# A post-norm attention and feed-forward layer on one Trainium2 core: turning tiles in quadrants of 32 on VectorE in place of TensorE transposes

## The reference

```python
local  = softmax(mask(q k^T / 4)) v                       # window of 128, per head
pooled = x.reshape(B, 64, 8, D).mean(axis=2)              # chunk means
lat    = softmax(mask(rq rk^T / 4)) rv                    # 64 latents, 4 heads
remote = lat @ rout_w + rout_b
gate   = sigmoid(local @ gl_w + remote_h @ gr_w)          # one value per token and head
mixed  = gate * local + (1 - gate) * remote_h
x1 = layernorm(x + mixed @ out_w + out_b)
h  = gelu(ternary_linear(x1, w_up))                       # rms norm, ternary weights
y  = layernorm(x1 + ternary_linear(h, w_down))
```

## Time and profile before

| | us |
|---|---|
| median of 3 runs | 1155.28 |
| lowest, highest | 1149.62, 1156.93 |
| the profiled execution: its own time | 1154.15 |
| the profiled execution: its span | 1152.4 |

### The profile page before, as it was taken

One profiled execution on the slowest core, in us unless ns is written; L12 is line 12 of the kernel. 1 busy time (PEld: TensorE's weight loads), 2 busy tenths in 40 slices (PEclk: granted clock), 3 DMA queues, 4 the chain that ended last, 5 costly groups with the idle time before them and its releaser, 6 DMA issues.

```text
span 1152.4 us, 37627 instructions
## 1 busy us (share of the span) xinstructions
PE 1019.2 (88%) x15616; PEld 642.4 (56%) x15616; DVE 902.5 (78%) x2119; ACT 682.4 (59%) x1076; POOL 698.0 (61%) x874
## 2 busy tenths in 40 slices
PE   5878999999999999999999999999999999986855
PEld 2445565655556565655656565565656555564533
DVE  6688888887887988787888888788788878875445
ACT  2425666656666665666666565666666566664523
POOL 7216675656667576566757565566756565673744
PEclk9889999999999999999999999999999999996877
DMA  7740604325060423416061331616042250600000
GB/s 219 204 125 14 193 21 120 87 77 148 32 193 23 145 61 104 121 42 182 24 167 56 113 94 59 166 33 187 28 131 77 85 139 33 174 23 20 2 19 18
DMA packets 46662, 108.18 MB, mean 94 GB/s; under 512 B 7542, under 2 KB 26486, under 8 KB 43382
## 3 DMA queue, kind: packets, MB, share of 16 engines
q1 hardware_dynamic: 46348, 105.78, 31.9%
q10 hardware_dynamic: 144, 0.00, 0.0%
HBM read 71.58 MB, written 34.08 MB: 92 GB/s over the span
## 4 chain that ended last, share of the span: by engine, by line
PE 44%; DVE 28%; ACT 16%; issue 5%; POOL 3%; DMA 2%; SPq 1%; DVEq 0%; POOLq 0%; ACTq 0%
PE oacc L1459 8%; PE work L1537 7%; PE oacc L1480 6%; PE work L1398 5%; PE scores L1439 4%; ACT Pt L792 4%; PE work L1469 3%; DVE Pt L974 3%; DVE nmax L1048 3%; DVE x L1111 2%; DVE rem L1115 2%; PE scores L1377 2%; ACT hbuf L828 2%; PE work L1403 2%; DVE oT L1176 2%
## 5 line engine op out<-in xcount | busy, mean ns | idle before, releaser
L792 ACT ACTIVATE Pt<-scores 128x1024 f32<-128x1024 f32 (+1 forms) x256 | 228.6, 915 | 104.5 <-PE oacc L1459 63.8
L1048 DVE TENSOR_REDUCE nmax<-work 128x3 f32<-128x480 f32 x352 | 218.1, 637 | 25.2 <-PE work L1403 20.0
L656 POOL TENSOR_TENSOR h_lo<-hbuf,h_hi 128x512 f16<-128x512 f32 x128 | 148.2, 1158 | 130.7 <-DVE h_hi L1170 130.7
L628 POOL TENSOR_SCALAR_AFFINE_SELECT Pt<-Pt 128x512 f32<-128x512 f32 x256 | 166.8, 652 | 91.2 <-ACT Pt L792 90.0
L615 POOL TENSOR_TENSOR parts<-Pt,parts 128x512 bf16<-128x512 f32 x64 | 72.9, 1157 | 138.2 <-ACT parts L728 138.2
L1459 PE MATMUL oacc<-Pt,Vp 128*32 128x256 f32 (+1 forms) x2048 | 150.2, 360 | 5.8 <-DVE ytok L1192 2.7
L1398 PE MATMUL work<-Ks,Qs 98*32 98x160 bf16 x4096 | 139.8, 235 | 11.4 <-DVE nmax L1048 7.4
L1439 PE MATMUL scores<-Qs,Ks 100*32 100x160 bf16 (+4 forms) x4096 | 114.8, 230 | 23.5 <-ACT Pt L792 15.9
L1480 PE MATMUL oacc<-wdn_t,h_hi 128*128 128x256 f16 x512 | 118.2, 273 | 5.6 <-POOL h_lo L656 5.6
L632 POOL TENSOR_SCALAR_AFFINE_SELECT Pt<-Pt 128x512 f32<-128x512 f32 x192 | 122.0, 635 | 0.0
L1297 PE MATMUL scores<-xT,wqk 128*128 128x512 f32 x256 | 114.9, 602 | 6.1 <-DMA xT<-x_t 6.1
(11 more groups left out here) (158 smaller groups left out, 1952.9 us busy)
## 6 DMA issues: line engine op xcount, KB each, us to landing
parts_scratch<-parts SPq DMA_DIRECT2D x96, 256.0 KB, 4.5
Qs<-parts_scratch SPq DMA_DIRECT2D x96, 256.0 KB, 4.7
Ks<-parts_scratch SPq DMA_DIRECT2D x96, 256.0 KB, 4.9
xT<-x_t SPq DMA_DIRECT2D x16, 512.0 KB, 6.6
xres<-x SPq DMA_DIRECT2D x16, 512.0 KB, 7.2
y<-ytok SPq DMA_DIRECT2D x16, 512.0 KB, 3.4
nat<-up_t SPq DMA_DIRECT2D x1, 1024.0 KB, 9.6
nat<-down_t SPq DMA_DIRECT2D x1, 1024.0 KB, 11.8
```

The lines of the kernel that those rows point to most:

```text
L628: ins = pool.affine_select(out=pt[:, :, 0:P], in_=pt[:, :, 0:P], compare_op=ALU.is_gt, fill=0.0, base=0, pattern=[[0, 4], [1, P]], channel ...
L656: pool.tensor_tensor(h_lo[:, t % NR, :], hbuf[:, t % 2, :], h_hi[:, t % NR, :], ALU.subtract).then_inc(h_lo_ready, 1)
L792: nc.scalar.activation(Pt[:, u % NPT, :, 0:w], scores[:, slot, :, :].rearrange("p k (h q) -> p (k h) q", h=2)[:, :, 0:w], ACT.Exp, scale=S ...
L1048: nc.vector.tensor_reduce(nmax[:, :, :].rearrange("p b h -> p (b h)")[:, first:first + n], work[:, slot, 0:n * BAND].rearrange("p (h c) -> ...
```

## The change

Five things change together.

1. **Turning.** VectorE's own transpose, which turns each 32 x 32 block of a tile by itself, takes the place of TensorE's. `take_o` turns `oacc` straight out of PSUM into `o_q` (no ScalarE copy, no "O" step, no use of a `work` slot); `mixed` is turned in halves of 256 tokens into `mixT`; the remote part comes feature-major from `REMOTE` (5 products in place of 4), ScalarE copies it out with its bias, and VectorE turns it; the row maxima are turned and split by VectorE (`split_maxima`). The rows of `out_w` and the columns of `rout_w` are permuted on the host to fit. `move_max` now issues 16 small DMAs, SBUF to SBUF, in place of two through DRAM.
2. **Gate.** The exponential and two reciprocals become a tanh and one reciprocal. GpSimd multiplies the remote part (two operations of 128 x 512) while VectorE multiplies the local part.
3. **Order.** OUT comes after three QK products, OUT+1 after the fourth; MIX_T is gone; LAT_RQ comes after OUT+1.
4. **Normalisation.** The last layer norm's four blocks are applied by ScalarE (`normalise_before`) in the second half, in a buffer `y2` of its own, and the store follows.
5. **Chunk sums.** They are taken one sequence earlier, on VectorE after UP+6; `xT` is loaded one sequence earlier too.

```diff
@@ the order by hand
-    ("F", GATE), ("P", QK), ("P", QK + 1), ("P", QK + 2), ("P", QK + 3), ("F", MIX_T),
-    ("P", LAT_RQ), ("F", OUT), ("P", LAT_RKV), ("F", OUT + 1), ("P", VALUES), ("P", LAT_SCORES), ("F", NORM),
+    ("F", GATE), ("P", QK), ("P", QK + 1), ("P", QK + 2), ("F", OUT), ("P", QK + 3),
+    ("F", OUT + 1), ("P", LAT_RQ), ("P", LAT_RKV), ("P", VALUES), ("P", LAT_SCORES), ("F", NORM),
...
+POOL_AT = ("F", UP + 6)
+NORMALISE_AT = {("F", GATE): (0, 1), ("P", QK + 2): (2, 3)}
@@ SyncE, move_max
+                wait_alone(sp, nmax_split, count(s, 1, 0))
+                for j in range(2):
...
+                    for g in range(NG):
+                        quadrant = slice(g * GT, (g + 1) * GT)
+                        for k in range(2):
+                            sp.dma_start(row[:, k, :, quadrant], nmax_pair[quadrant, j, k * GT:(k + 1) * GT]
+                                         ).then_inc(nmax_in[s.par], 16)
@@ GpSimd, f_step
+                        pool.tensor_tensor(of_half, of_half, ng.unsqueeze(3).to_broadcast([P, KT, G32, HD]),
+                                           ALU.mult).then_inc(mix_part, 1)
@@ ScalarE
+                if k == REMOTE:
...
+                    for i in range(2):
+                        bank, n = p_use(s, R_REM + i)
+                        act.wait_ge(p_full[bank], n + 1)
+                        for t in range(KT):
+                            ins = nc.scalar.activation(remT[:, t, i * HALF:(i + 1) * HALF],
+                                                       p_bank(bank)[:, t * HALF:(t + 1) * HALF], ACT.Identity,
+                                                       bias=brem[:, t:t + 1])
...
+            def normalise_before(s, b):
+
+                if b == 0:
+                    act.wait_ge(fin_ready, count(s, 1, -1))
+                nc.scalar.activation(y2[:, b, :], y2[:, b, :], ACT.Identity, scale=fin[:, 0, b:b + 1],
+                                     bias=fin[:, 1, b:b + 1]).then_inc(y_ready, 1)
@@ VectorE
+                if k == REMOTE:
+                    dve.wait_ge(rem_copied, count(s, 2, 0))
+                    for t in range(KT):
+                        ins = nc.vector.transpose(rem[:, s.par, t, :, :].rearrange("p b d -> p (b d)"), remT[:, t, :])
+                    ins.then_inc(rem_turned, 1)
...
             def take_o(s, hg):
 
-                slot, k = work_use(s, "O", hg)
-                dve.wait_ge(w_full[slot], k + 1)
-                nc.vector.tensor_copy(
...
+                dve.wait_ge(pv_done, count(s, NU, NB * hg + NB - 1))
+                nc.vector.transpose(o_q[:, hg // 2, :, hg % 2, :],
+                                    oacc[:, hg % 2, :].rearrange("p (b d) -> p b d", d=GT)).then_inc(o_taken, 1)
...
+                    for i in range(2):
+                        dve.wait_ge(mix_part, count(s, 2, i))
+                        done(nc.vector.tensor_tensor(mixed[:, i, :, :], mixed[:, i, :, :],
+                                                     of_half(rem[:, s.par, :, :, :], i).rearrange(
+                                                         "p t b d -> p t (b d)"), ALU.add))
+                        nc.vector.transpose(mixT[:, i, :, :].rearrange("p t n -> p (t n)"),
+                                            mixed[:, i, :, :].rearrange("p t n -> p (t n)")).then_inc(mixT_in, 1)
...
+                    if (phase, k) == POOL_AT and s.third_next().exists:
+                        pool_chunks(s.third_next())
```

More of the change, by code:

```diff
@@ L799, in f_step @@
                     act.wait_ge(gate_z, count(s, 1, 0))
-                    nc.scalar.activation(gate[:, 1, :, :], gate[:, 0, :, :], ACT.Exp, scale=-1.0
+                    nc.scalar.activation(gate[:, 1, :, :, :], gate[:, 0, :, :, :], ACT.Tanh, scale=0.5
                                          ).then_inc(gate_e, 1)
-                if k == MIX_T:
-                    for t in range(KT):
-                        act.wait_ge(mix_T, count(s, KT, t))
-                        nc.scalar.activation(mixT[:, t, :], oacc[:, t, :], ACT.Copy).then_inc(mixT_in, 1)
                 if NORM <= k < NORM + 2:
@@ L841, in body @@
                         weights(s, u)
-                    if u >= 6 and (u - 6) % NB == 0 and (u - 6) // NB < HG - 1:
-                        copy_o(s, (u - 6) // NB)
-                    if not s.last:
-                        for t in range(2):
-                            if u == T_AT[t]:
-                                max_high(s.next(), t)
-                copy_o(s, HG - 1)
                 later = s.second_next()
                 for phase, k in SECOND_HALF:
+                    if (phase, k) in NORMALISE_AT and not s.first:
+                        for b in NORMALISE_AT[phase, k]:
+                            normalise_before(s, b)
                     if phase == "F":
@@ L876, in _ @@
             over_sequences(body)
+            for b in range(NB):
+                normalise_before(Seq(B, 0, B // 2), b)
         @block.vector
@@ L1119, in f_step @@
-                    add_parts(NB - 1)
+                    dve.wait_ge(o_taken, count(s, HG, HG - 1))
+                    z, e, ng, r, a, half_r = (gate[:, j, :, :, :].rearrange("p t b m -> p (t b m)")
+                                              for j in range(6))
+                    of_heads = o_q[:, :, :, :, :].rearrange("p t b m d -> p (t b m) d")
+                    done(nc.vector.tensor_tensor(a, of_heads[:, :, VN],
+                                                 dead[:, :, :, :].rearrange("p t b m -> p (t b m)"), ALU.add))
@@ new lines, in f_step @@
+                    done(nc.vector.reciprocal(r, a))
+                    done(nc.vector.tensor_tensor(a, of_heads[:, :, HD], r, ALU.mult))
+                    dve.wait_ge(rem_turned, count(s, 2, 1))
+                    for t in range(KT):
+                        of_t = [gate[:, j, t, :, :].rearrange("p (i b) m -> p i b m", i=2) for j in (0, 4)]
+                        remote = remg[:, s.par, :, :].rearrange("p b (i r) -> p i b r", i=2)
+                        ins = nc.vector.tensor_tensor(of_t[0], of_t[1], remote[:, :, :, 2 * t:2 * t + 2], ALU.add)
@@ L1123, in f_step @@
                         dve.wait_ge(xres_done, count(s, NB, NB - 1))
-                        if not s.first:
-                            dve.wait_ge(y_out, count(s, 1, -1) * 16)
                     t = k - OUT
@@ L1186, in f_step @@
                     dve.wait_ge(x1_ready, count(s, NB, NB - 1))
-                    done(nc.vector.tensor_scalar(rs[:, 3, :], rs[:, 2, :], 1e-8, None, ALU.add))
-                    done(nc.vector.reciprocal(rs[:, 2, :], rs[:, 3, :]))
+                    done(nc.vector.tensor_scalar(hr[:, 2, :], hr[:, 1, :], 1e-8, None, ALU.add))
+                    done(nc.vector.reciprocal(hr[:, 3, :], hr[:, 2, :]))
+                    if not s.first:
+                        dve.wait_ge(y_out, count(s, 1, -1) * 16)
                     dve.wait_ge(down_done, count(s, FT, FT - 1))
@@ L1231, in body @@
                         ternary_down((2, 5, 8).index(u))
-                    if not s.last:
-                        for t in range(2):
-                            if u == T_AT[t]:
-                                max_low(s.next(), t)
+                    if u == A_STEPS and not s.last:
+                        split_maxima(s.next())
                 later = s.second_next()
@@ L1463, in weigh @@
                 mm.then_inc(pv_done, 1)
-            def transpose_o(s, hg):
-                pe.wait_ge(oT_ready, count(s, HG, hg))
-                slot = work_bank(s, "O", hg)
-                for b in range(NB):
-                    mm = nc.tensor.transpose(work[:, slot, b * P:(b + 1) * P], oT[:, b * P:(b + 1) * P],
-                                             ident[:, :])
-                mm.then_inc(w_full[slot], 1)
             def down(s, f):
```

383 lines of the change are left out of this document (197 added, 186 removed).

## The result

The changed kernel takes 1204.86 us (median of 4 runs, 1202.42 to 1210.18), the kernel before 1154.97 in the same sitting: ratio 1.0446, 95% interval 1.0396 to 1.0496. It is slower by 4.5%; the forecast was 3.4% faster. The profiled execution of after has a span of 1204.1 us, that of before 1152.4.

A forecast was written before the change was run, and what follows sets the result against it. TensorE holds some 93% of every stage, with VectorE and GpSimd close behind. Per sequence 1.3 + 2.2 - 1.4 = 2.1 us, 27.3 over thirteen; with the last three and the start 37.9, so 1154.15 becomes 1116 us; range 1088 to 1150.

The forecast's parts named there:

- The gate: From the last PV to the first up product: 2.2 us gained per sequence, by an earlier start and a shorter VectorE chain.
- two products of 512 at 0.65 each: VectorE's chain in the gate: its two products were to take 0.65 us each.
- GpSimd's products ... take 1.16 each: Gate: GpSimd's two products with the remote part, 1.16 us each, done before VectorE adds them.
- the second half of mixT at 577.4: Gate: VectorE's chain delivers the second half of `mixT` at 577.4 us; the last PV ends at 570.3.
- the 1.8 that VectorE was to gain there: Gate: VectorE free at 577.4 us where it was at 579.20, 1.8 us gained.
- The wait of 0.5: Gate: TensorE does three q and k products until 575.6, then waits 0.5 us for the projection.
- I take 1.3: Attention: 1.3 us gained per sequence, at most 1.5, as the stage can't go below 21.1 of 22.62.
- End of the feed-forward: Added waits make the column sums 1.4 us later per sequence; 2.8 with slow transposes, 0.7 with fast ones.
- The transpose: VectorE's transpose of 512 columns, unseen in the earlier trace: taken as 0.70 us, ends 0.45 and 1.24.
- TensorE's busy sum: Sign of being right in the later profile: TensorE's busy sum near 945 us; transposes worth 78.8 us go.
- the rival of slow transposes: VectorE's transposes pass every element twice, 1.24 us per 512 columns: 1173 us, deciding from about 0.98; chance 0.09.
- some other new wait that eats the gain: Anywhere in the kernel: an unnamed new wait uses up the gain; no size given; chance 0.10.

The follow-up runs named there:

- run 1: The changed kernel with both products of the remote part moved from GpSimd back to VectorE, behind its own two: 1186.4 us.
- run 9: The changed kernel with the fourth q and k product before the projection, chunk sums behind UP+3, remote products on VectorE half by half: 1141.0 us.
- run 4: The changed kernel with three unused 128x512 products on TensorE filling the wait for `mixT` ahead of the projection: 1196.2 us.
- run 5: The changed kernel with two unused TensorE products filling the waits around the down product of UP+6, at the end of the feed-forward: 1196.4 us.
- run 11: The kernel of run 9 plus five DMAs through DRAM for the maxima and ScalarE's |w| passes behind the first remote copies: 1128.9 us.
- run 12: The kernel of run 11 with the remote part's gate column, one ScalarE copy and one VectorE transpose, moved behind UP+7: 1127.5 us.
- run 6: The changed kernel with VectorE's chunk sums put behind UP+3 in place of UP+6: 1190.8 us.
- run 8: The changed kernel with ScalarE's two passes over |w| in the prologue put behind the first remote part's copies: 1199.6 us.

## Why the prediction was wrong

- **The gate** failed, in the step "two products of 512 at 0.65 each" beside "GpSimd's products ... take 1.16 each": I priced each engine from rows in which it worked alone and laid them side by side. They take 2.98 us together, not 1.3, and the small sum 0.71, not 0.27. So "the second half of mixT at 577.4", 7.1 us after the last PV, is 9.3 in after, and of the 1.8 that VectorE was to gain there is at most 0.3 in any run: free of the gate after 8.6 us in run 1 and 9.0 in run 9, where before needed 8.9. That is why even the repaired gate saves 0.4 us, not 2.2.
- **The wait of 0.5** for the projection is 2.7. I had named under 1 us as the sign of being right. Putting the projection ahead of the fourth product turned VectorE's delay into TensorE's idle time; with the order undone alone the gate costs nothing over before. I had no term for the clock in it: 0.75 us per gate (run 4).
- **Attention**: "I take 1.3" was right for the mechanism. With the clock kept in nearly all windows it is 1.4 or 1.5 less (runs 9 and 5). In after it is 0.4, and the clock falls behind the waits at the end of the feed-forward (none of it when they are filled). I priced those waits at their own length only.
- **End of the feed-forward**: +1.4 forecast, +1.17 measured, by the steps named: ScalarE's copies, then VectorE's pile.
- **The transpose** (the rival with the highest price): 705 ns for 512 columns, my 0.70. The Trainium skill (Vector Engine (DVE) Microarchitecture Reference, section 3.8) says "Pipelined to sustain one element per cycle per lane". The trace agrees in so far as the addition over as many elements takes about as long, 682.
- **TensorE's busy sum**: forecast near 945, measured 985.4 in after and 969.4 in run 9. I added the groups' busy times, 78.8, but matrix products overlap in the trace: without the three lines TensorE's busy time in before is 954.8, only 64.4 less. And the remote part's products take 30.1 us, 6.5 more than before, not 5.9. The sum of the forecast did not hang on it.
- **Slips**: the rival of slow transposes decides from 1.00 us on, not 0.98 (0.70 + 0.54 x 2.1 / 3.8); and "no operation in rows 6 takes more than 1.4 ns per element" holds for VectorE only: L615 on GpSimd takes 2.3, L733 on ScalarE 1.8.
- **Start and end**: Where no cover is left, the small DMAs were to cost "1 to 2 us each" in the first and the last sequence. That was too little. SyncE needs 10.0 us for 16, and the last scores wait 12.1 us for them (4.1 before): 6 us in sequence 14 alone. And I didn't see GpSimd's 7 us stall in sequence 0, which the new dependence on GpSimd exposed. The first PV starts 9.1 us later than before (91.8 to 82.7), where I had 1.5 for the whole start; runs 11 and 12 win 3.8 to 3.9 of it back.
- **The chances**: "some other new wait that eats the gain" had 0.10, and it was two of them, each with the clock on top.

What stays open: why a cure for one wait leaves more windows of the other stage below full clock (8 in runs 4 and 5, 9 in run 6, against 6); where run 8's gain lies; 5 us of the later start; and what GpSimd's stall of 7 us in sequence 0 is.

## What to carry to other kernels

Don't price work given to GpSimd from rows in which it ran alone: look whether VectorE then has operations with two SBUF inputs, and if so add the two engines' times instead of laying them side by side. Look in the trace for a place where both happen to run; here before had one. One input alone doesn't clear an operation either: transposes, reciprocals and maxima were not held up here, but casts out of SBUF were (below). When a wait on TensorE grows, price it twice, with its length and with the clock of the products behind it; and fill it by order, with work that is due anyway. Work moved off a busy engine pays only if the chain that replaces it is shorter at the point where the next engine picks up.

## What the runs showed of the hardware

- VectorE with two SBUF inputs and GpSimd's tensor_tensor, means in after: 0.69 us alone, 1.53 beside it (128x512); 0.26 alone, 0.71 beside it (128x64). GpSimd pays too: 2.52 for its two products in the middle, 2.06 in sequence 0, where VectorE was idle beside the first.
- VectorE's cast from fp32 to f16 (`h_hi<-hbuf`, 128x512, one SBUF input) takes 0.41 us on average where GpSimd is idle (91 times in after) and 0.81 where it is busy (37 times); before has 0.42 and 0.82. So the 537 ns of the earlier trace rows is a mixture. The maxima's reduction out of PSUM takes 0.64 idle and 0.63 beside GpSimd's masks.
- Attention behind two waits of TensorE of 0.6 and 0.7 us had a mean granted clock of 0.86 to 0.93 in 6 of 14 sequences, and in none when they were filled. Products whose result nobody uses made the kernel 0.7% faster.
- A DMA of 32 partitions with 64 bytes each occupies SyncE for 0.60 us on average in after (10.0 for 16 in a row): as long as the reads of 256 KB back into the stacks (0.58 and 0.59), and longer than the writes of 256 KB (0.41) and the loads of 512 KB (0.40 and 0.44).
